# The end of set-up in another order: step 0 of a quantised feed-forward kernel interleaved with input pair 1

## The reference, cut to what matters

```python
def fp4_linear(x, w):
    xq = fp4_quant_dequant(x)      # blocks of 16: scale = max|x| / 6, values on the grid 0, .5, 1, 1.5, 2, 3, 4, 6
    wq = fp4_quant_dequant(w)
    return jnp.einsum('bsk,nk->bsn', xq, wq)

xn = _layernorm(x)
s = causal_conv(xn, k) + xn * D    # k: 128 taps, built from Lambda, log_dt, W; written here in short
h = _silu(fp4_linear(xn, w_gate)) * fp4_linear(xn, w_up)      # 704 wide
g = _silu(fp4_linear(h, w_down))
return x + s * g
```

## Time and profile before

| | |
|---|---|
| median of 3 runs | 572.89 us (572.12 to 573.24) |
| profiled execution, its own time | 570.88 us |
| span of the trace | 568.8 us |
| PE busy | 477.2 us, 84% of the span |
| DVE busy | 530.7 us, 93% |
| ACT busy | 409.2 us, 72% |
| POOL busy | 212.0 us, 37% |

### The profile page before, as it was taken

The page is one execution under the profiler, slowest core; times in us unless marked ns, Lnnn a source line. Parts: engine busy times, 40 slices in busy tenths (PEclk is TensorE's granted clock), DMA queues, the critical chain, the costliest instruction groups (busy, mean ns, idle before and its releaser), DMA issues.

```text
span 568.8 us, 13319 instructions
## 1 busy us (share of the span) xinstructions
PE 477.2 (84%) x4981; PEld 332.1 (58%) x4981; DVE 530.7 (93%) x685; ACT 409.2 (72%) x583; POOL 212.0 (37%) x316
## 2 busy tenths in 40 slices
PE   0003474777999999999999999999999999999996
PEld 0000342344555567777777777777777777776675
DVE  6999975898999999999999999999999999999987
ACT  6949758799999976666666666667676666666554
POOL 1499601444555551111111111123233333237770
PEclk9999869889999999999999999999999999999999
DMA  5990002242222135353535353535444353526998
GB/s 162 350 314 1 1 19 93 92 103 94 92 93 94 56 93 165 96 146 100 148 94 167 94 167 93 165 97 145 117 125 135 114 149 112 150 75 124 191 175 177
DMA packets 101954, 70.80 MB, mean 124 GB/s; under 512 B 8864, under 2 KB 101536, under 8 KB 101792
## 3 DMA queue, kind: packets, MB, share of 16 engines
q1 hardware_dynamic: 94624, 62.73, 37.5%
q0 software_dynamic: 7280, 7.34, 8.5%
HBM read 61.28 MB, written 16.12 MB: 136 GB/s over the span
## 4 chain that ended last, share of the span: by engine, by line
PE 63%; DVE 25%; issue 7%; ACT 4%; DMA 0%; SPq 0%; DVEq 0%; ACTq 0%
PE ps L1325 32%; PE ps L1343 10%; PE ps L1345 5%; PE ps L1334 5%; PE ps L1358 4%; PE ps L1362 4%; DVE work L1033 4%; DVE work L949 3%; DVE work L944 3%; DVE work L973 2%; DVE sm L911 2%; PE ps L1313 2%; DVE xh L1011 1%; DVE xh L1001 1%; DVE work L981 1%
## 5 line engine op out<-in xcount | busy, mean ns | idle before, releaser
L1325 PE MATMUL ps<-wgu,work 128*128 128x512 f16 (+1 forms) x1152 | 243.8, 367 | 21.6 <-DVE work L973 20.8
L1325 PEld LDWEIGHTS ps<-wgu,work 128*128 128x128 f16 x1152 | 110.1, 99 | 132.9 <-issue 20.4
L682 ACT ACTIVATE work<-ps,con 128x704 f32<-128x704 f32 x64 | 54.2, 847 | 95.4 <-PE ps L1325 95.4
L1343 PE MATMUL ps<-wdh,work 128*128 128x256 f16 x704 | 87.2, 272 | 0.3 <-ACT work L677 0.2
L677 ACT COPY work<-ps 128x1408 f16<-128x1408 f16 x64 | 84.8, 1325 | 1.6 <-PE ps L1334 1.6
L944 DVE SCALAR_TENSOR_TENSOR work<-work 128x960 f32<-128x960 bf16 (+2 forms) x67 | 72.0, 1112 | 5.0 <-ACT work L697 5.0
L548 POOL TENSOR_TENSOR gbuf<-gbuf,xh 128x256 f32<-128x256 f32 (+1 forms) x42 | 37.8, 929 | 94.0 <-DVE work L957 86.7
L930 DVE TENSOR_TENSOR work<-work,ps 128x960 f32<-128x960 f32 (+2 forms) x67 | 71.5, 1105 | 1.2
L949 DVE SCALAR_TENSOR_TENSOR work<-work 128x1920 f16<-128x1920 bf16 (+3 forms) x36 | 69.7, 1936 | 1.2
L1343 PEld LDWEIGHTS ps<-wdh,work 128*128 128x128 f16 x704 | 65.2, 98 | 7.6 <-ACT work L677 0.4
L911 DVE TENSOR_REDUCE sm<-work 128x120 f32<-128x1920 f32 (+2 forms) x33 | 68.0, 2059 | 1.3
(11 more groups left out here) (155 smaller groups left out, 682.7 us busy)
## 6 DMA issues: line engine op xcount, KB each, us to landing
work<-kpad SPq DMA_DIRECT2D x64, 512.0 KB, 3.8
gbuf<-u_rev SPq DMA_DIRECT2D x4, 2048.0 KB, 17.9
work<-L_attn_u SPq DMA_DIRECT2D x32, 256.0 KB, 2.9
out<-gbuf POOLq DMA_DIRECT2D x7, 1024.0 KB, 11.5
work<-L_attn_u SPq DMA_DIRECT2D x1, 1024.0 KB, 5.3
out<-gbuf SPq DMA_DIRECT2D x3, 256.0 KB, 2.2
work<-L_ffn_w_down SPq DMA_DIRECT2D x1, 704.0 KB, 7.7
work<-L_ffn_w_gate SPq DMA_DIRECT2D x1, 640.0 KB, 4.6
```

The source lines that it names most:

```text
L1325: last = T.matmul(p_gu[:, a:b], xT[par][:, t, c, :], wgu[:, part, c % 2, a:b], start=(n == 0), stop=(n == len(todo) - 1))
L1343: T.matmul(dst, hT[t][:, c, :], wdh[:, c, :], start=(c == 0), stop=False)
```

## The change

It moves instructions on DVE, ACT, PE and POOL between about 78 and 104 us of the trace before; none is added or taken away. SP's program stays.

- DVE: the first operations of step 0 (the block maxima of input pair 2, then its scales and its division) now stand inside set-up's work on pair 1, `h_mult(0)` stands before `x_second(1)`, and the rest of step 0 is written out after `powers`. Maxima and scales become two functions.
- ACT: `x_norm(2)`, the second half's scales and `a_scale(7)` stand ahead of `square(-1)` and `silu_gate(0)`. `square(0)` and `silu_gate(1)` stand between the copies of the down weights 8 to 10 and 11 to 12. `x_copy(1)` and `x_norm(3)` stand ahead of those last copies, the filter's two operations behind `a_high(1)`.
- PE: `reverse(1)` moves ahead of `gate_up(0)`, the filter's first small transpose to right behind it, `transposed_down(2)` behind the second one, and `x_transpose(1)` ahead of `transposed_down(3)` and `(4)`. A wait for the last weight copies ahead of step 1 goes; `a_high(0)` on ACT still has it.
- POOL: the subtraction for the filter's low part moves from ahead of `tables(0)` to behind `tables(1)`.

```diff
@@ gpsimd
-            pool.wait_ge(k_split, 2)
-            nc.gpsimd.tensor_tensor(kl, kt, kh, ALU.subtract).then_inc(k_split, 1)
...
                 tables(it, it < NP - 2, it >= 1)
+                if it == 1:
+                    pool.wait_ge(k_split, 2)
+                    nc.gpsimd.tensor_tensor(kl, kt, kh, ALU.subtract).then_inc(k_split, 1)
@@ scalar
             nc.scalar.copy(dn_hi[1], dn_src).then_inc(w_h, 1)
+            x_norm(2, 0)
+            input_scales(1)
+            norm_scales(1)
+            a_scale(7)
             square(-1, 0, True, False, 0)
             act.wait_ge(w_lo, 3)
             act.wait_ge(w_h, 4)
             silu_gate(0)
-            input_scales(1)
-            norm_scales(1)
             weights_out(range(8, 11))
-            x_norm(2, 0)
-            a_scale(7)
+            square(0, 1, True, False, 0)
+            silu_gate(1)
+            x_copy(1, 1)
+            x_norm(3, 1)
             weights_out(range(11, 13))
+            a_high(0, 2)
+            a_high(1, 2)
             act.wait_ge(k_sc, 1)
             nc.scalar.activation(kt, kt, ACT.Copy, scale=mxs).then_inc(k_split, 1)
             act.wait_ge(k_split, 1)
             nc.scalar.copy(kh, kt).then_inc(k_split, 1)
-            x_copy(1, 1)
-            for it in range(PEEL):
+            for it in range(1, PEEL):
@@ vector
             x_first(1)
+            x_scales()
+            largest(0, 1, True, False)
             largest_of_rows(k_row1, 1, k_one, p_row1)
-            x_scales()
+            h_mult(0, 0, 0)
             x_second(1)
-            h_mult(0, 0, 0)
             x_parts(1, 1)
+            scales(0, True, False)
+            inverse(1, True, False)
             dve.wait_ge(k_all, 1)
             powers(slice(3, 4), p_all1)
...
+            round_a(0, 1, 0, XH)
+            last = round_b(1, XH, own.n)
+            dve.wait_ge(tb_p, 1)
+            last.then_inc(x_r, 1)
+            x_parts(2, 0)
+            h_mult(1, 1, 0)
...
-            for it in range(PEEL):
+            for it in range(1, PEEL):
@@ tensor
+            reverse(1)
             pe.wait_ge(w_ca, 8)
             gate_up(0, 0, 0, 1)
-            reverse(1)
+            pe.wait_ge(k_max, 1)
+            T.transpose(p_row1[0:1, :], mxi[:, 3:4], id32).then_inc(k_row1, 1)
...
             transposed_down(1)
-            pe.wait_ge(k_max, 1)
-            T.transpose(p_row1[0:1, :], mxi[:, 3:4], id32).then_inc(k_row1, 1)
-            transposed_down(2)
             pe.wait_ge(k_one, 1)
             T.transpose(p_all1[:, 3:4], row[0:1, :], id32[0:1, 0:1]).then_inc(k_all, 1)
+            transposed_down(2)
             gate_up(1, 1, 0, None)
+            pe.wait_ge(con_ok, 1)
+            x_transpose(1, 1)
             pe.wait_ge(w_ca, 9)
             transposed_down(3)
             pe.wait_ge(w_ca, 10)
             transposed_down(4)
-            pe.wait_ge(con_ok, 1)
-            x_transpose(1, 1)
-            pe.wait_ge(w_ca, 13)
```

More of the change, by code:

```diff
@@ L710, in y_copy, with step @@
                                      scale=con[:, C_CONV:C_CONV + 1]).then_inc(cv_e, 1)
-            def step(it, par, x, xt, xn, gu, ch, td, a2=False, cv=0, c0=None, td1=True, first=True, more=None):
+            def step(it, par, x, xt, xn, gu, ch, td, a2=False, cv=0, c0=None, td1=True, more=None):
                 if td:
                     h_copy(it * 2 - 4, 0)
-                if a2 and first:
+                if a2:
                     a_scale(it * 2)
-                if gu and first:
+                if gu:
                     silu_gate(it * 2)
@@ L734, in step @@
                     scaled = (2, 6, 10)[it] if isinstance(it, int) and it < 3 else it + (NT // 8 + 1)
-                    if not first:
-                        a_high(it * 2, scaled)
                 if more is not None:
@@ L743, in step @@
                 if a2:
-                    if first:
-                        a_high(it * 2, scaled)
+                    a_high(it * 2, scaled)
                     a_high(it * 2 + 1, scaled)
@@ L858, in _ @@
             nc.scalar.copy(kh, kt).then_inc(k_split, 1)
-            x_copy(1, 1)
-            for it in range(PEEL):
-                step(it, it % 2, True, it >= 1, True, True, it >= 1, it >= 2, a2=True, td1=it >= 3, first=it >= 1,
-                     more=(None, 9, 13, None)[it])
+            for it in range(1, PEEL):
+                step(it, it % 2, True, True, True, True, True, it >= 2, a2=True, td1=it >= 3, more=(None, 9, 13, None)[it])
                 if it in (1, 2):
@@ L912, in scales_and_largest, with scales @@
                                          apply_absolute_value=True))
+            def scales(it, x, ch):
+                cols = columns(x, ch)
                 own.settle()
@@ L1163, in _, with step @@
             V.tensor_scalar(mxs, minv[:, 3:4], XS, None, ALU.mult).then_inc(k_sc, 1)
-            def step(it, par, x, gu, ch, first=True):
+            round_a(0, 1, 0, XH)
[4 more added lines that the diff above has]
+            h_mult(1, 1, 0)
+            def step(it, par, x, gu, ch):
                 pp = 1 - par
                 cols, parted = columns(x, ch), pieces(x, ch)
-                scales_and_largest(it, pp, x, ch)
+                largest(it, pp, x, ch)
+                scales(it, x, ch)
                 inverse(pp, x, ch)
-                if gu and first:
+                if gu:
                     h_mult(it * 2, 0, par)
@@ L1189, in step @@
                     h_mult(it * 2 + 1, 1, par)
[L1191 removed]
+            for it in range(1, PEEL):
                 start = own.n
[L1193 removed]
+                step(it, it % 2, True, True, True)
             per_step = own.n - start
@@ L1220, in finish @@
                                 ).then_inc(f_t, 1)
-            scales_and_largest(NP, 1, False, True)
+            largest(NP, 1, False, True)
+            scales(NP, False, True)
             inverse(1, False, True)
```

3 lines of the change are left out of this document (1 added, 2 removed).

## The result

The changed kernel takes 564.77 us (median of 4 runs, 564.18 to 565.95) against 572.5 (median of 4 runs, 570.53 to 573.24): a ratio of 0.9869, with a 95% interval of 0.9844 to 0.9894. The profiled execution went from 570.88 to 564.18 us and its span from 568.8 to 562.2: 6.7 and 6.6 us, where the prediction's sum had 8.3.

A forecast was written before the change was run, and what follows sets the result against it. DVE, ACT and PE waited for one another in turn at set-up's end, with each later step released by the one before. Starting step 1 earlier gave -8.3 us: 570.88 to 562.6 profiled, plus 2.0 for the median, 564.6; range 563.4 to 567.6.

The forecast's parts named there:

- Set-up's end: Before step 1: waits vanish, DVE starts step 1 at 92.5 to 92.7 instead of 100.83, 8.1 to 8.3 us earlier.
- The sum: Whole kernel: ACT's earlier start is carried through steps 1 to 3 and DVE's hides under its wait; -8.3 us.
- POOL's part: Set-up's end: `tables(0)` takes under 2.4 us, done by 89.9; only SP's filter store waits for the moved subtraction.
- The clock: PE's `gate_up(3)` after about 3.1 us idle: cost bounded by 0 and 2.04 us, taken as 0.
- the nearest row: Earlier PE trace: `gate_up` after 2.29 us of idle time ran at 3.74 us, none lost.
- `h_mult` at 138.14: Later step on DVE: this operation starts at 129.8 instead, still waiting over 1 us for ACT.
- rival 1: PE's clock: `gate_up(3)` at 1.2 GHz throughout, gain 5.3, or `gate_up(1)` slow, gain 6.4; chance 0.05 each.
- Rival 2: ACT, its slack gone from 90.2 us, is the new bound: price 2 to 3 us, gain 5.3 to 6.3; chance 0.10.
- Rivals 3: Steps 1 to 8: an engine with its own schedule absorbs the gain, about 573 us; chance 0.03.
- 4: ACT's `x_norm(3)`: a late input load stalls everything; slower, +4.9 us, 577.8 us; chance 0.03.

The follow-up runs named there:

- Kernels 1: Kernel before with only the filter's two small transposes on PE moved earlier; 568.48 us, ratio 0.9943.
- kernel 2: Kernel before with only ACT's second half and POOL's filter subtraction moved as in the change; 571.39 us, ratio 0.9973.
- 9: Kernel before plus the moves of Kernels 1 and kernel 2 together, without the rest of the change; 566.93 us, ratio 0.9902.
- 6: Changed kernel with POOL's `tables(1)` between `a_low(0)` and `a_low(1)`, later `a_low` and the subtraction moved behind the wait for `x_parts(3)`; 563.96 us, ratio 0.9864.
- kernel 4: Changed kernel with POOL's `tables(1)` ahead of both `a_low`; 566.41 us, ratio 0.9900.
- kernel 11: Changed kernel with the alterations of 6 and kernel 10 together; 563.62 us, ratio 0.9834.
- kernel 10: Changed kernel with `a_scale(15)` on ACT moved from step 2 to the end of step 3; 563.61 us, ratio 0.9852.
- the control: Kernel 5: the changed kernel, unaltered, timed again; 565.39 us, ratio 0.9877 against the kernel before.
- kernels 8: Kernel before with 36 extra matmuls on PE, results unused, ahead of the loop over steps; 573.32 us, ratio 1.0024.

## Why the prediction was right, and where not

*Set-up's end: right.* Step 1 at 92.38 (92.5 to 92.7 forecast), silu(2) at 98.14 without idle time (98.4), `h_mult(2)` at 99.00 (99.3), ACT's remaining idle time 0.52 (0.4), `gate_up(1)` at 85.11 with 3.74 us (85.3, 3.74). Walking the three lists with the old durations was good to 0.3 us over 10 us of program. Kernels 1, 2 and 9 show that no part does it alone.

*The sum: 1.6 us too high (8.3 against 6.7 by profiled executions).* The step of it that failed is "The lists of steps 1 to 3 are unchanged, so the shift of ACT, 8.3 us, is carried through", together with POOL's part, of which I costed `tables(0)` and the subtraction and not `tables(1)`. ACT's list is unchanged, but DVE's place against POOL's is not. DVE came 8.45 us earlier and POOL, which waits for ACT's `a_high` before its `a_low`, by only 5.04 (94.59 against 99.63 in the earlier trace rows). So `tables(1)`, which stands behind both `a_low` in both kernels, fell out of the division and into the rounding. DVE waited 0.99 us, and L987 took 0.48 longer beside the subtraction. `h_mult(3)`, `gate_up(4)` and silu(4) followed late, with 1.52 us of new idle time on ACT. The shift by start of step, 1 to 8: 8.45, 7.18, 7.07, 7.09, 7.08, 6.74, 6.74, 6.62. The first 1.27, from 8.45 to 7.18, are shown to be this meeting: it goes away when `tables(1)` runs earlier (6), turns against DVE in another order (4), and comes back in step 3 (11). That it hangs on both operands being in SBUF agrees with the profiles of before, after, 2, 4, 6, 9 and 11; I varied the order, not the operands, so it is not shown apart from the DVE instruction's kind.

*What stays open.* Of the smaller losses, the 0.11 us of step 2 are what `gate_up(4)` took more than before (5.03 against 4.92). The 0.34 and 0.12 us in steps 5 and 7 are open. In step 5 DVE waits 0.53 us for PE's transposes where it waited 0.18 before, and I did not follow it further.

*The clock: 0 was right for this execution, and in part by luck.* `gate_up(3)` took 3.74 us after 3.35 us of idle time, as the nearest row had it. But idle time alone does not sort the rows: after 3.36 us the same matmuls took 5.42 us in kernel 10 and 6.45 in kernel 11; after 2.29 us `gate_up(1)` took 3.74 us in the kernel before and 5.35 in kernel 2; and `gate_up(2)` took 3.73 and 5.21 us in two executions of the changed kernel. Taking the nearer of two rows gave no ground for a price. Nor is the price the same everywhere: the control hid a slow `gate_up(2)`, while a slow `gate_up(4)` costs in full. In ten of the thirteen profiles step 2 on DVE lasted what `gate_up(4)` took plus 9.62 or 9.63 us (14.54 us for 4.92 before, 14.65 for 5.03 after, 15.68 for 6.05 in kernel 4). The other three are kernels 8, 10 and 11, where `gate_up(3)` took over 5 us. What decides over the level is open.

*`h_mult` at 138.14: half right.* It still waits for ACT, 1.53 us as before, but starts at 131.05 and not 129.8, by the 1.3 us lost.

*The rivals.* Neither half of rival 1 came about in the profiles of the changed kernel; kernels 10 and 11 show that a slow `gate_up(3)` can come about at this very place. Rival 2, ACT as the bound, holds at silu(2) by the trace (no idle time) and at silu(6) by kernel 10, but was priced as an extra wait, and the wait came from POOL. Rivals 3 and 4 did not occur. A fourth gain-eater, two engines shut out of one another, was missing from my list. With its 1.3 us I would have said 7.0 for the spans.

*Why the median was hit: luck.* By medians the gain is 7.7 us, by profiled executions 6.7. The profiled execution of before, at a mean granted clock of 0.979, lies 2.0 us under the median of the first three runs (572.89); that of after, at 0.985, 0.6 under its median. I added the 2.0 to both. Kernel 5 shows what such an offset is made of: 1.1 us between two executions of one kernel, 0.73 in set-up and 0.39 by `gate_up(4)`. The forecast of 564.6 against 564.77 thus holds a gain taken 1.6 too high and an offset taken 1.4 too high, which cancel.
